# Attention in an adaptive-norm transformer block: the order of one unit's matmuls, written out in four blocks of two key tiles

## The chip, the core and the metric

The kernel runs on one core of one Trainium2 chip. The metric is the device time of one execution in microseconds (us). The kernel before takes 4075.78 us, the median of three runs (4074.69 to 4077.95).

## The reference

A transformer block (8 sequences of 1024 tokens, 512 features, 16 heads of 32) with modulated layer norms, and a modulated RMS norm behind it. Everything is float32. What the change touches is the softmax attention and its projection:

```python
h = layernorm(x, g1, be1) * (1.0 + scale_msa) + shift_msa
q, k, v = split_heads(h @ Wqkv + bqkv)                 # (8, 16, 1024, 32) each
attn = softmax(einsum('blhd,bmhd->bhlm', q, k) * 32 ** -0.5)
out = einsum('bhlm,bmhd->blhd', attn, v).reshape(8, 1024, 512)
x = x + gate_msa * (out @ Wproj + bproj)
h = layernorm(x, g2, be2) * (1.0 + scale_mlp) + shift_mlp
x = x + gate_mlp * (gelu(h @ W1 + b1) @ W2 + b2)
return rmsnorm(x) * (1.0 + scale) + shift              # scale, shift from a quantised projection
```

## The kernel before

Three stages follow each other: norm and QKV (to about 645 us), attention with its projection (to about 2560 us), MLP and the last norm. Each engine has one instruction stream, written out in the same nested loops, and semaphores tie the streams together. Only the attention stage and its seams are changed.

**A unit** of attention is four heads (128 features) of one sequence and one half of its queries (512 columns); there are `NU` = 64 units, `u` below. A unit has eight key tiles of 128 keys, `kt`. Its pieces, with the letter that the order strings use for them:

- `m`, a **maximum**: one 128x512 matmul of scores with the queries on the output's partitions (`pe_maximum`, L527) into one of **three** PSUM banks `SMAX`, and a VectorE reduction over it (`dve_maximum`, L817). 32 of them give the softmax shift of one later unit. A maximum may be written only when the reduction three places earlier in the ring has read its bank (`pe.wait_ge(dve_smax, at.turn - 2)`).
- `!`, the **send**: PE transposes the 16 maxima (L535, one turn of the same ring), VectorE negates them in two parts (L833, L836), and SyncE writes them as two more rows of the next unit's `q_stack`.
- `s`, a **score**: the same product with keys on the partitions and the shift in it (`pe_score`, L989) into one of three banks `ST`; ScalarE takes its exponential into `probs` (L1121). 32 per unit, four (one per head) for each key tile.
- **values** (`pe_values`, L1002): probabilities times V, four matmuls of 32 output rows each, one per head, that share the array in column tiles. As fp32 they run in two passes, so that the profile has 8 records for one key tile. **Denominators** (`pe_denominators`, L1018) are the same form against ones: number 0 and 1 for the last two key tiles, number 2 for `prob_sum`, the sum over the six others that GpSimd adds up (L1235, L1241; five additions of 128x2048 for a unit). "Column-tile products" below are both of these; a unit has eight values and three denominators.
- the **projection** of one token tile, 12 matmuls of 128x512 (L1029, L1031, L1033) into `DEN_BANK`, `PROJ_LAG` = 9 units late. ScalarE and GpSimd split its operand (`act_project` L1086, `pool_project` L1212), and VectorE gates its result (`dve_gate`, L1172).
- ScalarE empties the value bank (`act_weigh`, L1093); VectorE turns the denominators round, inverts, spreads and applies them (L1139, L1145, L1150, L1162).

**The order before** stands in a table for four steps of two key tiles, each in two halves:

```python
ORDER = (("mssm*mssm", "mssmm*mssmm"), ("mssm*mssm", "mssm*ssm"),
         ("mssm*ssm", "mssm*ssm"), ("mssm*!mssm", "mssmm*mssm"))
```

At a `*` PE does the step's other work (`pe_step_work`): two values; two denominators; one denominator and one value; one value three times; two values; and in the last half the whole projection. So the column-tile products of a unit stand in seven groups. `LEAD` = 9 maxima of a unit run ahead of its predecessor's send.

Of the kernel before, what the change touches and what calls it, by code (L numbers as in the profile page):

```python
# [7 lines left out]
def build_block(nc, t, out):  # L8
# [33 lines left out]
    STEPS = KT // 2  # L42
    LAST = STEPS - 1


    ORDER = (("mssm*mssm", "mssmm*mssmm"), ("mssm*mssm", "mssm*ssm"),
             ("mssm*ssm", "mssm*ssm"), ("mssm*!mssm", "mssmm*mssm"))
    LEAD = sum(x.count("m") for x in ORDER[-1])
# [11 lines left out]
    with whole:  # L60
# [104 lines left out]
        probs = [s2(f"probs{i}", [P, GH, 2, CH]) for i in range(3)]  # L165
# [104 lines left out]
        def slot(u, s):  # L270
            return (u * STEPS + s) % len(probs)

        def maxima_at(u, n):

            return u * N_MAX + n < NU * N_MAX

        def sums_done(u, s):
            return 5 * u + (1, 3, 5)[s]
# [135 lines left out]
        def ring_of_send(u):  # L414

            if u == 0:
                return N_MAX
            return min(N_MAX * (u + 1) + 2, N_MAX * NU) + u
# [510 lines left out]
        def sp_attention(sp):  # L929
# [7 lines left out]
            for u in range(NU):  # L937
# [16 lines left out]
                for s in range(STEPS):  # L954
                    for hs in range(2):
                        for what in ORDER[s][hs]:
                            if what == "!":
                                if u + 1 < NU:
                                    send_max(sp, u + 1)
                            elif what == "*" and (s, hs) == (0, 0):  # L960
                                if u and tile - 1 >= 0:
                                    store_gated(sp, tile - 1)
                                if half == 0 and G + 1 < NGRP:
                                    if u:
                                        sp.wait_ge(pe_pv, 8 * u)
                                    load_values(sp, G + 1)
# [13 lines left out]
        def pe_score(pe, u, s, h, j):  # L980
            G = u // NCH
            kt = 2 * s + j
            n = u * 32 + s * 8 + h * 2 + j
            if s == 0 and h == 0 and j == 0:
                pe.wait_ge(a_m[u % 3], 32 * (u // 3 + 1))
                pe.wait_ge(pool_ones, min(G, 1) + 1)
# [5 lines left out]
        def pe_values(pe, u, s, j):  # L992
            G = u // NCH
            kt = 2 * s + j
            if j == 0:
                pe.wait_ge(act_exp, u * 32 + s * 8 + 8)
# [4 lines left out]
            for h in range(GH):  # L1001
                i = pe.matmul(psum[h * HD:(h + 1) * HD, PV_BANK, :],  # L1002
                              v_group[G % 2][:, kt, h * HD:(h + 1) * HD],
                              probs[slot(u, s)][:, h, j, :], start=kt == 0, stop=kt == KT - 1)
            i.then_inc(pe_pv, 1)

        def pe_denominators(pe, u, n):
            term = prob_sum[u % 2] if n == 2 else probs[slot(u, LAST)][:, :, n, :]
            if n == 0:

                if u - PROJ_LAG >= 0 and u < NU:
# [3 lines left out]
            if n == 2:  # L1015
                pe.wait_ge(pool_sum, sums_done(u, 2))
# [4 lines left out]

        def pe_project(pe, n, bank):
            hi, lo = attn_hi[n % 2], attn_lo[n % 2]
            pe.wait_ge(act_ahi, n + 1)
            pe.wait_ge(pool_alo, n + 1)
            if n == 0:
                pe.wait_ge(dve_wprojlo, 1)
            for k in range(KD):
                pe.matmul(psum[:, bank, :], hi[:, k, :], wproj_hi[:, k, :], start=k == 0,  # L1029
                          stop=False)  # L1030
                pe.matmul(psum[:, bank, :], hi[:, k, :], wproj_lo[:, k, :], start=False,  # L1031
                          stop=False)
                i = pe.matmul(psum[:, bank, :], lo[:, k, :], wproj_hi[:, k, :], start=False,  # L1033
                              stop=k == KD - 1)
            i.then_inc(pe_proj2, 1)

        def pe_step_work(pe, u, s, hs):
            tile = u - PROJ_LAG
            if (s, hs) == (0, 0):
                if u:  # L1040
                    pe_values(pe, u - 1, LAST, 0)
                    pe_values(pe, u - 1, LAST, 1)
            elif (s, hs) == (0, 1):
                if u:
                    pe_denominators(pe, u - 1, 0)
                    pe_denominators(pe, u - 1, 1)
            elif s in (1, 2):
                if (s, hs) == (1, 0) and u:
                    pe_denominators(pe, u - 1, 2)
                pe_values(pe, u, s - 1, hs)  # L1050
            elif (s, hs) == (3, 0):
                pe_values(pe, u, 2, 0)
                pe_values(pe, u, 2, 1)
            elif tile >= 0:
                pe.wait_ge(dve_attn, u)
                pe_project(pe, tile, DEN_BANK)

        def pe_attention(pe, at):

            pe.wait_ge(dve_evict1, NC * 12)  # L1060
            for u in range(NU):
                for s in range(STEPS):
                    for hs in range(2):
                        n = 0
                        for what in ORDER[s][hs]:
                            if what == "s":
                                pe_score(pe, u, s, 2 * hs + n // 2, n % 2)
# [733 lines left out]
```

## Time and profile before

| | before |
|---|---|
| median of three runs | 4075.78 us |
| the profiled execution | 4073.34 us, span 4071.6 us |
| granted TensorE clock, mean | 0.993 |
| PE busy | 3995.4 us (98%) |
| VectorE, ScalarE, GpSimd busy | 2473.4, 1795.4, 1923.4 us |
| TENSOR_REDUCE of a maximum | 2048 times, 683 ns |
| exponential | 2048 times, 599 ns |
| GpSimd addition for `prob_sum` | 256 + 64 times, 4593 and 4589 ns |

PE means matmuls, PEld the loads of their stationary operands, which overlap them. Matmuls are pipelined: one of 128x512 is recorded with about 390 ns and the next starts about 230 ns after it, so that work on PE is counted from start to start. A matmul whose operand load came late is recorded with about 500 ns: it really starts about 0.11 us after its record does. An idle time of PEld with a releaser behind it is a wait of the load, and PE shows it only as such a longer record or a longer step to the next.

### The profile page before, as it was taken

The numbers are of one execution on the slowest core, as the hardware profiler recorded it, in microseconds if no ns is written. First come the engines' busy times: TensorE is split into PE (matmuls) and PEld (weight loads), VectorE is DVE, ScalarE is ACT, GpSimd is POOL, SyncE is SP. The second block draws the span as 40 slices with busy tenths as digits, with TensorE's granted clock in tenths as the row PEclk, the third lists the DMA queues.
The fourth block names the chain that finished last, engine by engine and source line by source line (L and its number), as shares of the span: only waits on it lengthen the run. The fifth ranks groups of instructions, "written<-read, shape, count | busy, mean of one in ns | idle before, by whom it ended". The sixth has DMA issues, their size and how long they took to land.

```text
span 4071.6 us, 51447 instructions
## 1 busy us (share of the span) xinstructions
PE 3995.4 (98%) x19723; PEld 2648.5 (65%) x19723; DVE 2473.4 (61%) x4020; ACT 1795.4 (44%) x3220; POOL 1923.4 (47%) x530
## 2 busy tenths in 40 slices
PE   8999999999999999999999999799999999999998
PEld 6778875445455455454455544588888888888886
DVE  3665557887777777777777775234445443344442
ACT  2222224665565555655555556333333333333332
POOL 1000005888788787887887878632211122231111
PEclk9999999999999999999999999999999999999999
DMA  5444463233323323323323330411110111201110
GB/s 199 175 173 176 183 210 102 53 73 76 75 64 82 78 53 84 76 55 84 74 65 74 74 78 26 142 55 42 34 42 34 42 39 50 62 34 42 34 42 21
DMA packets 184993, 323.70 MB, mean 80 GB/s; under 512 B 14452, under 2 KB 53428, under 8 KB 184748
## 3 DMA queue, kind: packets, MB, share of 16 engines
q1 hardware_dynamic: 184748, 320.41, 27.7%
q8 instruction: 156, 2.56, 0.3%
q14 instruction: 89, 0.73, 0.1%
HBM read 201.77 MB, written 117.54 MB: 78 GB/s over the span
## 4 chain that ended last, share of the span: by engine, by line
PE 94%; DVE 1%; DMA 1%; issue 1%; POOL 1%; ACT 1%; SPq 0%; POOLq 0%; ACTq 0%; DVEq 0%
PE psum L527 13%; PE psum L989 13%; PE psum L1002 12%; PE psum L428 10%; PE psum L430 9%; PE psum L429 9%; PE psum L1510 6%; PE psum L1514 6%; PE psum L1512 6%; PE psum L1018 4%; PE psum L1029 1%; PE psum L1031 1%; PE psum L1033 1%; PE psum L1472 1%; PE psum L463 1%
## 5 line engine op out<-in xcount | busy, mean ns | idle before, releaser
L817 DVE TENSOR_REDUCE max_part<-psum 128x1 f32<-128x512 f32 x2048 | 1298.6, 683 | 351.6 <-PE psum L527 340.8
L1121 ACT ACTIVATE probs<-psum 128x512 f32<-128x512 f32 x2048 | 1071.6, 599 | 686.1 <-PE psum L989 683.8
L1241 POOL TENSOR_TENSOR prob_sum<-prob_sum,probs 128x2048 f32<-128x2048 f32 x256 | 1175.8, 4593 | 111.7 <-ACT probs L1121 92.5
L1643 DVE TENSOR_TENSOR g_parts<-g_full,g_parts 128x512 fp32r<-128x512 f32 x256 | 311.7, 1217 | 776.0 <-ACT g_parts L1552 776.0
L527 PE MATMUL psum<-k_stack,q_stack 96*128 96x512 f32 x2048 | 758.2, 419 | 3.0 <-DVE max_part L817 1.3
L989 PE MATMUL psum<-q_stack,k_stack 98*128 98x512 f32 x2048 | 675.7, 411 | 4.9 <-DMA q_stack<-negmax_lo 2.5
L527 PEld LDWEIGHTS psum<-k_stack,q_stack 96*128 96x128 f32 x2048 | 387.5, 189 | 295.2 <-DVE max_part L817 235.9
L989 PEld LDWEIGHTS psum<-q_stack,k_stack 98*128 98x128 f32 x2048 | 372.1, 189 | 290.9 <-ACT probs L1121 250.2
L1548 ACT ACTIVATE g_full<-psum,cols 128x512 f32<-128x512 f32 x256 | 176.5, 690 | 823.4 <-PE psum L430 823.0
L1710 POOL TENSOR_TENSOR y_out<-y_out,rows 128x512 f32<-128x512 f32 x64 | 82.4, 1289 | 947.4 <-DVE y_out L1681 947.4
L1002 PE MATMUL psum<-probs,v_group 128*32 128x512 f32 x4096 | 517.4, 600 | 0.9 <-ACT probs L1121 0.9
L1235 POOL TENSOR_TENSOR prob_sum<-probs 128x2048 f32<-128x2048 f32 x64 | 293.7, 4589 | 254.6 <-ACT probs L1121 254.6
L1510 PE MATMUL psum<-w_hi,g_parts 128*128 128x512 f32 x1024 | 406.0, 396 | 0.0
L428 PE MATMUL psum<-h_hi,w_hi 128*128 128x512 f32 x1024 | 402.5, 393 | 1.7 <-ACT g_parts L1552 1.7
L1512 PE MATMUL psum<-w_lo,g_parts 128*128 128x512 f32 x1024 | 403.5, 394 | 0.0
L1514 PE MATMUL psum<-w_hi,g_parts 128*128 128x512 f32 x1024 | 403.4, 394 | 0.0
L430 PE MATMUL psum<-h_hi,w_lo 128*128 128x512 f32 x1024 | 401.4, 392 | 0.0
L429 PE MATMUL psum<-h_lo,w_hi 128*128 128x512 f32 x1024 | 401.1, 392 | 0.0
L1002 PEld LDWEIGHTS psum<-probs,v_group 128*32 128x32 f32 x4096 | 100.2, 108 | 231.7 <-issue 145.6
L428 PEld LDWEIGHTS psum<-h_hi,w_hi 128*128 128x128 f32 x1024 | 192.3, 188 | 48.5 <-issue 3.8
L1514 PEld LDWEIGHTS psum<-w_hi,g_parts 128*128 128x128 f32 x1024 | 192.3, 188 | 45.2
L1512 PEld LDWEIGHTS psum<-w_lo,g_parts 128*128 128x128 f32 x1024 | 192.4, 188 | 43.8
(152 smaller groups left out, 4731.7 us busy)
## 6 DMA issues: line engine op xcount, KB each, us to landing
qk_parts<-qk_out SPq DMA_DIRECT2D x128, 512.0 KB, 2.8
k_stack<-qk_parts SPq DMA_DIRECT2D x96, 512.0 KB, 7.0
q_stack<-qk_parts SPq DMA_DIRECT2D x192, 256.0 KB, 9.4
x_in<-in_x SPq DMA_DIRECT2D x16, 1024.0 KB, 5.4
v_rows<-v_out SPq DMA_DIRECT2D x64, 256.0 KB, 2.0
v_group<-v_rows SPq DMA_DIRECT2D x32, 512.0 KB, 12.1
gated_attention<-gated SPq DMA_DIRECT2D x64, 256.0 KB, 4.6
x<-in_x SPq DMA_DIRECT2D x16, 1024.0 KB, 7.9
```

The lines of the kernel that those rows point to most:

```text
L428: pe.matmul(dst, lh, rh, start=n == 0, stop=False)
L429: pe.matmul(dst, lh, rl, start=False, stop=False)
L430: last = pe.matmul(dst, ll, rh, start=False, stop=n == len(terms) - 1)
L527: pe.matmul(psum[:, SMAX[at.turn % 3], :], q_stack[u % 3][0:PARTS, h, i * P:(i + 1) * P], k_stack[G % 2][0:PARTS, h, kh * CH:(kh + 1) * CH ...
L817: dve.reduce_max(max_part[:, n:n + 1], psum[:, SMAX[at.turn % 3], :], AX.X).then_inc(dve_smax, 1)
L989: pe.matmul(psum[:, ST[n % 3], :], k_stack[G % 2][0:ROWS, h, kt * P:(kt + 1) * P], q_stack[u % 3][0:ROWS, h, :], start=True, stop=True).th ...
L1002: i = pe.matmul(psum[h * HD:(h + 1) * HD, PV_BANK, :], v_group[G % 2][:, kt, h * HD:(h + 1) * HD], probs[slot(u, s)][:, h, j, :], start=kt ...
L1121: act.activation(probs[slot(u, s)][:, h, j, :], psum[:, ST[k % 3], :], ACT.Exp, scale=SCALE).then_inc(act_exp, 1)
L1241: pool.tensor_tensor(prob_sum[u % 2][:, :, :], prob_sum[u % 2][:, :, :], probs[slot(u, s)][:, :, j, :], ALU.add).then_inc(pool_sum, 1)
L1510: pe.matmul(psum[:, ACC[m], :], gp[:, 0, cut], w2_hi[piece][:, at, :], start=i == 0, stop=False)
L1512: pe.matmul(psum[:, ACC[m], :], gp[:, 0, cut], w2_lo[piece][:, at, :], start=False, stop=False)
L1514: pe.matmul(psum[:, ACC[m], :], gp[:, 1, cut], w2_hi[piece][:, at, :], start=False, stop=i == KM - 1).then_inc(pe_down, 1)
```

## The change

The unit's order becomes one string of four blocks. Each block scores two key tiles and ends in all its column-tile products (`V` values, `D` denominators); the projection's products, `j`, stand one by one in the last block. The other letters place work of the other engines: `g` gate, `w` weigh, `a` `act_project`, `t r p n` turn, reciprocal, spread, normalise.

The send stands at the middle of the unit, so `LEAD` becomes 16. The probabilities have a ring of six single key tiles in place of three pairs, and values run two key tiles behind the scores (`PV_LAG`). The sums wait and run per key tile, and `pool_project` stands behind the second addition. In the seam to the MLP the first projection of the tail moves ahead of the denominators, and the second ahead of denominator 2.

```diff
-    ORDER = (("mssm*mssm", "mssmm*mssmm"), ("mssm*mssm", "mssm*ssm"),
-             ("mssm*ssm", "mssm*ssm"), ("mssm*!mssm", "mssmm*mssm"))
-    LEAD = sum(x.count("m") for x in ORDER[-1])
+    ORDER = ("msgmsmsmsamsmsmsmsVVDD", "mswmsmsmsmsmsmsmsVVD!", "msmstsmsrmspsmsmsVV",
+             "nmsmsmsmjsjmjsjmjsjmjsjmjsjmjmjVV")
+    LAST = KT - 1
+    SUMMED = KT - 2
+    AHEAD = 0
+    LEAD = N_MAX + AHEAD - "".join(ORDER).split("!")[0].count("m")
+    PV_LAG = 2
+    RING = 6
...
-        probs = [s2(f"probs{i}", [P, GH, 2, CH]) for i in range(3)]
+        probs = [s2(f"probs{i}", [P, GH, CH]) for i in range(RING)]
...
+                for what in "".join(ORDER):
...
+                    elif what == "V":
+                        if values >= PV_LAG:
+                            pe_values(pe, u, values - PV_LAG)
+                        elif u:
+                            pe_values(pe, u - 1, values - PV_LAG + KT)
+                        values += 1
+                    elif what == "D" and u:
+                        pe_denominators(pe, u - 1, dens)
+                        dens += 1
+                    elif what == "j" and u - PROJ_LAG >= 0:
+                        if products == 0:
+                            pe.wait_ge(dve_attn, u)
+                        pe_project_product(pe, u - PROJ_LAG, DEN_BANK, products)
+                        products += 1
...
+                        if h == 0 and k >= RING:
+                            pu, pk = divmod(k - RING, KT)
+                            act.wait_ge(pe_pv, k - RING + 1)
+                            if pk >= SUMMED:
+                                act.wait_ge(pe_den, 3 * pu + pk - SUMMED + 1)
+                            else:
+                                act.wait_ge(pool_sum, sums_done(pu, pk))
...
         def pe_tail(pe):
             at = TAIL[0]
-            pe_values(pe, NU - 1, LAST, 0)
-            pe_values(pe, NU - 1, LAST, 1)
-            pe.wait_ge(dve_gated, at)
+            for kt in range(KT - PV_LAG, KT):
+                pe_values(pe, NU - 1, kt)
+            pe.wait_ge(dve_smax, FIRST_TAIL)
+            pe_project(pe, at, tail_bank(at))
             pe_denominators(pe, NU - 1, 0)
             pe_denominators(pe, NU - 1, 1)
-            pe.wait_ge(dve_smax, FIRST_TAIL)
-            pe_project(pe, at, tail_bank(at))
+            pe_project(pe, at + 1, tail_bank(at + 1))
             pe_denominators(pe, NU - 1, 2)
```

On PE, a unit's start before (L527 maxima, L989 scores, L1002 values, L1018 denominators; a row's x8 counts matmuls in the program):

```order
L1002 MATMUL psum<-probs_116,v_group_103 32x512 x8
L527 MATMUL psum<-k_stack_111,q_stack_101 128x512
L989 MATMUL psum<-q_stack_112,k_stack_111 128x512 x2
L527 MATMUL psum<-k_stack_111,q_stack_101 128x512 x2
L989 MATMUL psum<-q_stack_112,k_stack_111 128x512 x2
L527 MATMUL psum<-k_stack_111,q_stack_101 128x512 x2
L1018 MATMUL psum<-probs_116,ones 32x512 x8
```

The same place on PE after the change, the end of the first block (L532 maxima, L992 scores, L1003 values, L1019 denominators):

```order
L532 MATMUL psum<-k_stack_100,q_stack_112 128x512
L992 MATMUL psum<-q_stack_102,k_stack_111 128x512
L532 MATMUL psum<-k_stack_100,q_stack_112 128x512
L992 MATMUL psum<-q_stack_102,k_stack_111 128x512
L1003 MATMUL psum<-probs_115,v_group_113 32x512 x4
L1003 MATMUL psum<-probs_116,v_group_113 32x512 x4
L1019 MATMUL psum<-probs_115,ones 32x512 x4
L1019 MATMUL psum<-probs_116,ones 32x512 x4
```

Before, products stood behind every four to six maxima and scores; now 16 of these run in strict alternation, and two values and two denominators follow together.

VectorE before, from the gate (L1172) to the send (L833, L836) and on to the next gate, with the runs of reductions (L817) between its other work:

```order
L817 TENSOR_REDUCE max_part<-psum 128x1 x9
L1172 TENSOR_TENSOR gated_125<-psum,gates_other 128x512
L817 TENSOR_REDUCE max_part<-psum 128x1 x10
L1139 STREAM_TRANSPOSE den_turned<-psum 128x512
L817 TENSOR_REDUCE max_part<-psum 128x1 x4
L1145 RECIPROCAL den_inv<-den_turned 128x16
L817 TENSOR_REDUCE max_part<-psum 128x1 x3
L1150 STREAM_TRANSPOSE psum<-den_inv 128x512
L817 TENSOR_REDUCE max_part<-psum 128x1 x3
L1162 TENSOR_TENSOR attn_last<-weighted_130,psum 128x512
```

VectorE after the change (L822 is the reduction, L1162 the gate, L838 and L841 the send, L1129, L1135, L1140 and L1152 turn, reciprocal, spread and normalise):

```order
L1162 TENSOR_TENSOR gated_128<-psum,gates_last 128x512
L822 TENSOR_REDUCE max_part<-psum 128x1 x15
L829 TENSOR_REDUCE max_q<-max_part 128x16
L838 TENSOR_SCALAR negmax_hi<-psum 16x128
L841 SCALAR_TENSOR_TENSOR negmax_lo<-psum,negmax_hi 16x128
L822 TENSOR_REDUCE max_part<-psum 128x1 x2
L1129 STREAM_TRANSPOSE den_turned<-psum 128x512
L822 TENSOR_REDUCE max_part<-psum 128x1
L1135 RECIPROCAL den_inv<-den_turned 128x16
L822 TENSOR_REDUCE max_part<-psum 128x1
L1140 STREAM_TRANSPOSE psum<-den_inv 128x512
```

The gate has moved behind the first maximum of the first block, and send, turn, reciprocal and spread have moved together into the third block, among six maxima.

## Rows read from the trace of the kernel before

**Rows 1.** The page: the chain that ended last, by engine.
```profile
PE 94%; DVE 1%; DMA 1%; issue 1%; POOL 1%; ACT 1%; SPq 0%; POOLq 0%; ACTq 0%; DVEq 0%
```
**Rows 2.** Timeline of PE: start us, us, engine line op, tiles, count.
```profile
2011.58 1.92 PE L1002 MATMUL psum<-probs,v_group 128*32 128x512 f32 x16
2013.44 0.50 PE L527 MATMUL psum<-k_stack,q_stack 96*128 96x512 f32 x1
2013.78 0.63 PE L989 MATMUL psum<-q_stack,k_stack 98*128 98x512 f32 x2
...
2022.32 0.63 PE L989 MATMUL psum<-q_stack,k_stack 98*128 98x512 f32 x2
...
2023.25 0.65 PE L989 MATMUL psum<-q_stack,k_stack 98*128 98x512 f32 x2
2023.74 0.39 PE L527 MATMUL psum<-k_stack,q_stack 96*128 96x512 f32 x1
2024.06 1.06 PE L1002 MATMUL psum<-probs,v_group 128*32 128x512 f32 x8
2025.06 0.74 PE L989 MATMUL psum<-q_stack,k_stack 98*128 98x512 f32 x2
...
2036.96 0.39 PE L1029 MATMUL psum<-wproj_hi,attn_hi 128*128 128x512 f32 x1
...
2039.45 0.39 PE L1033 MATMUL psum<-wproj_hi,attn_lo 128*128 128x512 f32 x1
```
**Rows 3.** Timeline of PE: a send in units 0, 1, 10 and 61.
```profile
669.65 0.28 PE L535 MATMUL psum<-ident,max_q 128*16 128x128 f32 x1
697.58 0.28 PE L535 MATMUL psum<-ident,max_q 128*16 128x128 f32 x1
951.32 0.28 PE L535 MATMUL psum<-ident,max_q 128*16 128x128 f32 x1
2485.75 0.28 PE L535 MATMUL psum<-ident,max_q 128*16 128x128 f32 x1
```
**Rows 4.** Timeline of VectorE, around one gate and one idle start.
```profile
2012.54 0.68 DVE L1172 TENSOR_TENSOR gated<-psum,gates_other 128x512 f32<-128x512 f32 x1
2013.97 3.19 DVE L817 TENSOR_REDUCE max_part<-psum 128x1 f32<-128x512 f32 x5 [0.75 <-PE psum L527]
...
2021.35 0.71 DVE L1139 STREAM_TRANSPOSE den_turned<-psum 128x512 f32<-128x512 f32 x1
```
**Rows 5.** Timeline of PE in unit 0: three maxima behind a full ring.
```profile
671.42 1.49 PE L527 MATMUL psum<-k_stack,q_stack 96*128 96x512 f32 x3
672.74 0.63 PE L989 MATMUL psum<-q_stack,k_stack 98*128 98x512 f32 x2
```
**Rows 6.** Timeline of VectorE at the same place, behind the send.
```profile
670.48 3.66 DVE L817 TENSOR_REDUCE max_part<-psum 128x1 f32<-128x512 f32 x6
```
**Rows 7.** Timeline of ScalarE: the weigh and four exponentials.
```profile
2013.57 0.60 ACT L1093 ACTIVATE weighted<-psum 128x512 f32<-128x512 f32 x1 [1.21 <-PE psum L1002]
2014.21 2.06 ACT L1121 ACTIVATE probs<-psum 128x512 f32<-128x512 f32 x4
```
**Rows 8.** Timeline of GpSimd over one unit.
```profile
2019.64 4.59 POOL L1235 TENSOR_TENSOR prob_sum<-probs 128x2048 f32<-128x2048 f32 x1 [4.30 <-ACT probs L1121]
2024.20 1.27 POOL L1212 TENSOR_TENSOR attn_lo<-attn_other,attn_hi 128x512 fp32r<-128x512 f32 x1
2026.76 18.66 POOL L1241 TENSOR_TENSOR prob_sum<-prob_sum,probs 128x2048 f32<-128x2048 f32 x4 [1.29 <-ACT probs L1121]
```
**Rows 9.** The waits, 1000 to 2400 us: who for whom, us, times, longest.
```profile
PEld psum L527 <- DVE max_part L817: 168.0, 323, 0.8
```
**Rows 10.** Timeline of PE, unit 63 and the seam behind it.
```profile
2520.00 0.86 PE L989 MATMUL psum<-q_stack,k_stack 98*128 98x512 f32 x3
...
2528.17 0.50 PE L989 MATMUL psum<-q_stack,k_stack 98*128 98x512 f32 x1 [0.22 <-ACT probs L1121]
...
2557.63 1.06 PE L1018 MATMUL psum<-prob_sum,ones 128*32 128x512 f32 x8
```

More of the change, by code:

```diff
@@ L953, in sp_attention @@
                     load_gates(sp, b)
[L954 to L966, printed above, removed]
+                values = 0
+                for what in "".join(ORDER):
+                    if what == "!" and u + 1 < NU:
+                        send_max(sp, u + 1)
+                    elif what == "V":
+                        values += 1
+                        if values == PV_LAG and half == 0 and G + 1 < NGRP:
+                            if u:
+                                sp.wait_ge(pe_pv, KT * u)
+                            load_values(sp, G + 1)
+                    elif what == "g" and tile >= 1:
+                        store_gated(sp, tile - 1)
         def load_gates(sp, b):
@@ L1020, in pe_denominators, with pe_project_product @@
             i.then_inc(pe_den, 1)
-        def pe_project(pe, n, bank):
[L1023 to L1056, printed above, removed]
+        def pe_project_product(pe, n, bank, m):
+            hi, lo = attn_hi[n % 2], attn_lo[n % 2]
+            if m == 0:
+                pe.wait_ge(act_ahi, n + 1)
+                pe.wait_ge(pool_alo, n + 1)
+                if n == 0:
+                    pe.wait_ge(dve_wprojlo, 1)
+            k, kind = divmod(m, 3)
+            left, right = ((hi, wproj_hi), (hi, wproj_lo), (lo, wproj_hi))[kind]
+            i = pe.matmul(psum[:, bank, :], left[:, k, :], right[:, k, :], start=m == 0,
+                          stop=m == 3 * KD - 1)
+            if m == 3 * KD - 1:
+                i.then_inc(pe_proj2, 1)
+        def pe_project(pe, n, bank):
+            for m in range(3 * KD):
+                pe_project_product(pe, n, bank, m)
         def pe_attention(pe, at):
@@ new lines, in act_attention @@
+                scores = 0
+                for what in "".join(ORDER):
+                    if what == "s":
+                        kt, h = divmod(scores, GH)
+                        k = u * KT + kt
+                        if h == 0 and k >= RING:
[5 more added lines that the diff above has]
+                                act.wait_ge(pool_sum, sums_done(pu, pk))
+                        n = k * GH + h
+                        act.wait_ge(pe_st, n + 1)
+                        act.activation(probs[slot(u, kt)][:, h, :], psum[:, ST[n % 3], :],
+                                       ACT.Exp, scale=SCALE).then_inc(act_exp, 1)
+                        scores += 1
+                    elif what == "w" and u:
+                        act_weigh(act, u - 1)
+                    elif what == "a" and tile >= 0:
+                        act_project(act, tile)
@@ L1380, in dve_tail @@
             dve.wait_ge(pe_den, 3 * NU)
[L1381 to L1382 removed]
+            dve.wait_ge(pool_sum, sums_done(NU - 1, SUMMED - 1))
+            for n, tile in enumerate(TAIL[2:], 2):
                 dve_gate(dve, tile, tail_bank(tile))
```

157 lines of the change are left out of this document (57 added, 100 removed).

## The prediction

> **What bounds the kernel now.** I read the page first: PE is busy for 98% of the span (the table above) and makes 94% of the chain that ended last [rows 1]. So only time on PE counts, and time of another engine only where it holds PE up. Next the sends, one per unit, as a clock: 951.32 to 2485.75 us is 51 units with a projection, 30.09 us each; 697.58 to 951.32 is eight without one and one with, so (253.74 - 30.09) / 8 = 27.96 for those [rows 3]. What fills a unit comes from the timeline of PE, start to start [rows 2].
>
> - Four maxima and scores from 2022.32 to 2023.25: 0.233 each. Projection: 11 steps from 2036.96 to 2039.45, 0.226 each.
> - A group of two column-tile products lasts 1.86 until the next matmul (2011.58 to 2013.44), a group of one 1.00 (2024.06 to 2025.06): 0.86 for one, and 0.14 once per group. The step into a group is 0.32 (2023.74 to 2024.06) and the first step behind one 0.34 (2013.44 to 2013.78, whose first record is 0.50 long, an operand load that could not run ahead), in place of 0.233. A group thus costs 0.09 + 0.14 + 0.105 = 0.33 beyond its products.
>
> The unit before: 64 x 0.233 + 12 x 0.226 + 11 x 0.86 + 7 x 0.33 = 14.9 + 2.7 + 9.45 + 2.3 = 29.4. The other 0.65 are waits that show only as long records and steps: the loads of maxima wait for a reduction 323 times and 168 us in 1400 us [rows 9], most of it ahead of time and so free.
>
> The Trainium skill (TensorEngine Tiling (Array Packing), Key Properties) says that changing the tiling mode drains the engine; by that rule alone fewer groups are a pure gain, and the sum would be rival A below. The same page (PSUM Bottleneck) warns that tiling speeds up TensorE and not the emptying of PSUM; the terms below, from rows, go that way.
>
> **The rule of the ring.** Three banks stand between PE and VectorE. Count a maximum from its effective start E (record plus 0.105 where it follows a group). Its reduction starts at E + 0.43: 2013.44 + 0.105 to 2013.97 [rows 2, 4]. One lasts 0.69 after an idle start, 0.67 to 0.68 in a queue; six take 3.66, so the step is (3.66 - 0.67) / 5 = 0.60 [rows 6]. The gate takes 0.68 [rows 4], in a queue one more step of 0.60. What does PE see when it waits? In unit 0 the third reduction ends at 670.48 + 1.20 + 0.67 = 672.35, and the matmul behind the third waiting maximum starts at 672.74 [rows 5, 6], so that the maximum's own E was 672.51: E of a maximum is at least F + 0.16, F the end of the reduction three turns earlier. Scores obey the same rule with ScalarE: step (2.06 - 0.60) / 3 = 0.49 [rows 7], and in unit 63 the fourth score of a run starts 1.19 after the first [rows 10], which is 0.43 + 0.60 + 0.16.
>
> A pair of maximum and score costs PE 0.47 and VectorE 0.60. A run of strict pairs therefore uses up three banks of slack and then goes at VectorE's pace. Before, a group stood behind every two or three maxima and gave VectorE its time back; now eight maxima run before one.
>
> **The change, block by block** (t from the block's first record, F and E as above; all other steps at 0.233).
>
> - Removed: three groups, 3 x 0.33 = -1.00 per unit, and the old waits, -0.65.
> - Block 1, eight pairs and the gate behind the first maximum. E1 = 0.105, reduction 0.54 to 1.23, gate from 1.14, second reduction 1.74 to 2.42, then F3, F4, F5 = 3.02, 3.62, 4.22. E5 = 2.58 instead of 1.97, E8 = F5 + 0.16 = 4.38 instead of 3.37. Wait: +1.0. The block is 4.38 + 0.23 + 0.32 + four products (1.86 + 2 x 0.86 = 3.57) = 8.5; VectorE is done at 6.0, so that each long group does empty its queue, but with nothing left to gain from it.
> - Block 2, eight pairs without the gate: F5 = 3.62, E8 = 3.78, +0.4. ScalarE's weigh stands behind the first exponential and pushes the second to 1.76 to 2.36; score 5 then waits for 2.52 instead of 2.22, score 7 for 3.50, and the block's last score is at 4.0 to 4.13 [rows 7]. That is +0.45 in all; length 7.1 with three products.
> - Block 3: the send takes the ring's first turn. Its first reduction starts 0.83 behind the transpose (669.65 to 670.48) [rows 3, 6], F1 = 1.50, F2 = 2.10, then the turn (0.71, rows 4) to 2.74 and F3 = 3.33. E6 must wait for it: 3.49 instead of 2.92. +0.57. The exponentials add nothing beyond it (score 6 at 2.52, inside the same wait). Length 5.9.
> - Block 4: normalise is done at 0.6, behind the third block's last reduction; the fourth maximum may start at 1.43 and would at 1.50; from there on a projection product stands between two pieces, 0.69 or more per maximum but for the last. No wait. 0.105 + 18 x 0.233 + 12 x 0.226 + 0.09 + 1.86 = 9.0.
>
> Sum 8.5 + 7.1 + 5.9 + 9.0 = 30.5, against 30.09: as a difference -1.00 - 0.65 + 1.0 + 0.45 + 0.57 = +0.37 to +0.40. Bounds: if the gate hid wholly (it would have to wait for nothing and cost no step) block 1 falls to 0.4, and the unit to -0.2; if the weigh and the turn each cost a full step more, it is +0.6. I take +0.38, since every term uses a duration that the rows show in the same engine state.
>
> In units 1 to 8 nothing is gated or projected: block 1 waits 0.4, block 4 has ten maxima in pairs (E10 = F7 + 0.16 = 4.97, wait +1.0, length 7.15), sum 28.06 against 27.96: +0.1 each.
>
> GpSimd: five additions and the split are 4.59 + 1.27 + 18.66 = 24.5 of a unit [rows 8]. From the unit's start: sum 1 from 5.7 to 10.3 (key tile 1's last exponential), sum 2 from 11.3, the split until 17.2, the rest until 31. The tile that needs the sum 5 buffer is scored at 30.5 + 10, the earliest other one (key tile 6 over tile 0) at 22 over 10.3. Slack of 9 or more; no wait. The split is done 4 ahead of the first `j` at 23. Keys and queries for the maxima two units on are now wanted at 15.6 instead of about 23 into a unit, but their loads leave SyncE some 3 us before its start, with the last score; the page has 7.0 and 9.4 us to landing. Free.
>
> **The seams.** LEAD moves seven maxima into the end of the QKV stage, where PE is the bound: 7 x 0.233 = +1.6. They come out of unit 62, whose last two blocks then run at ScalarE's pace (eight scores in a run: 3.27 + 0.32 instead of 3.92 with maxima), as all of unit 63. There GpSimd sets the end: its sums finish some 30.3 into unit 63, the split 1.3 later, then projection, two denominators, projection, denominator 2: done at about 40.6, against 38.7 from the same unit's first scores at 2520.0 to 2558.7, the last record's end [rows 10]. Everything behind hangs on that last one: +2.
>
> **Total.** 52 units x 0.38 = +19.8; unit 9 (no gate yet) -0.2; units 0 to 8 about +1.1; QKV end +1.6; seam +2. +24.3 on the profiled execution's 4073.34 (its span 4071.6 and 1.7 around it) is 4097.6. The median of the runs lies 2.4 above that execution, so I forecast **4100 us**, +0.6%; its own range is 4090 to 4112.
>
> **Rivals.**
>
> - A, faster: the saved groups count whole and the waits stay at 0.65. Mechanism: the load of the waiting maximum is taken while scores run, so that the ring's delay is absorbed; point of decision: it needs four banks' worth of slack, or reductions at 0.47 like the pair. For it: the old loads wait 168 us and PE shows almost nothing of it [rows 9]. Against: there a group follows within three maxima, and rows 5 show the wait in full when none does. Price -1.00 x 62 + 3.6 for the seams: 4017.
> - B, no change: a wait costs only until the release, with the load hidden (0.11 less). That takes 0.11 from three blocks, +0.05 per unit, with the seams +6 to +8: 4083. For it: several waits in a row could overlap; against: rows 5 and 10.
> - C, slower still: the third block's VectorE backlog reaches the fourth, and the projection waits for the normalise (needed by 1.7, done by 0.6 by my sum). If reciprocal and spread each wait 0.5 for the step before, block 3 waits 0.6 more: 4135. The rows of before have no such chain without maxima between.
>
> That the change does not do what it says is excluded: the program's order has the four groups and the single `j`.
>
> **Chances.** Forecast 0.68, A 0.12, B 0.12, C 0.08. A difference of 0.2% (8 us) is about what a measurement of this kernel can tell from none. Faster 0.14 (A, and some of B), same 0.12, slower 0.74. The range leaves out most of A and part of C: 4068 to 4120.
>
> **What would show it.** In the changed profile the sends of units 10 to 61 stand 30.4 to 30.5 apart; the eighth maximum of block 1 starts 4.3 to 4.4 behind the first, in records of about 0.5; block 2 about 7.1 long, block 3 5.9, block 4 9.0; reductions in block 1 in one queue with the gate, without idle time; loads of maxima that wait for reductions well over 168 us in 1400. If the sends stand 29.1 apart, the ring's rule fails and A is right. If the unit is right and the total is not, the seams are.

## The result, and the profile after

The changed kernel takes 4105.71 us (median of 4 runs, 4105.40 to 4106.81) against 4075.79 for the one before (4 runs): a ratio of 1.0073, with a 95% interval of 1.0056 to 1.0091. It is slower by 30 us, where 24 were forecast. The profiled execution took 4106.81 us with a span of 4105.0; its mean granted clock was 0.992.

The page: the span, the busy line, and the chain that ended last. PE is busy for the same 97 to 98% as before, but its share of the chain has gone from 94% [rows 1] to 87%, and VectorE's from 1% to 4%.

```profile
span 4105.0 us, 51828 instructions
PE 4001.0 (97%) x19723; PEld 2688.5 (65%) x19723; DVE 2439.9 (59%) x4020; ACT 1791.7 (44%) x3220; POOL 1920.1 (47%) x530
PE 87%; DVE 4%; issue 3%; ACT 2%; DMA 2%; POOL 1%; SPq 0%; ACTq 0%; POOLq 0%; DVEq 0%
```

The unit's pace, from the timeline of PE: the sends of units 10 and 61, and one in between from which the rows below go on. 2505.22 - 947.87 is 51 units of 30.54; before it was 30.09 [rows 3].

```profile
947.87 0.28 PE L540 MATMUL psum<-ident,max_q 128*16 128x128 f32 x1
...
1986.14 0.28 PE L540 MATMUL psum<-ident,max_q 128*16 128x128 f32 x1
...
2505.22 0.28 PE L540 MATMUL psum<-ident,max_q 128*16 128x128 f32 x1
```

One unit's blocks, from the timeline of PE (L532 maxima, L992 scores, L1003 values, L1019 denominators, L1033 projection). Block 3 runs from the send at 1986.14 to 1992.01, block 4 to 2001.06, block 1 of the next unit to 2009.58.

```profile
1992.01 0.50 PE L532 MATMUL psum<-k_stack,q_stack 96*128 96x512 f32 x1
...
1999.21 1.92 PE L1003 MATMUL psum<-probs,v_group 128*32 128x512 f32 x16
2001.06 0.50 PE L532 MATMUL psum<-k_stack,q_stack 96*128 96x512 f32 x1
2001.40 0.40 PE L992 MATMUL psum<-q_stack,k_stack 98*128 98x512 f32 x1
...
2003.54 0.50 PE L532 MATMUL psum<-k_stack,q_stack 96*128 96x512 f32 x1 [0.35 <-DVE max_part L822]
...
2005.33 0.50 PE L532 MATMUL psum<-k_stack,q_stack 96*128 96x512 f32 x1
2005.68 0.40 PE L992 MATMUL psum<-q_stack,k_stack 98*128 98x512 f32 x1
2006.01 1.92 PE L1003 MATMUL psum<-probs,v_group 128*32 128x512 f32 x16
2007.75 1.90 PE L1019 MATMUL psum<-probs,ones 128*32 128x512 f32 x16
2009.58 0.50 PE L532 MATMUL psum<-k_stack,q_stack 96*128 96x512 f32 x1
```

The fifth maximum starts 2.48 behind the first, the eighth 4.27, each in a record of 0.50. VectorE in the same block, from its timeline: one reduction, the gate, seven reductions, with no idle time between them.

```profile
2001.60 0.69 DVE L822 TENSOR_REDUCE max_part<-psum 128x1 f32<-128x512 f32 x1 [1.69 <-PE psum L532]
2002.21 0.68 DVE L1162 TENSOR_TENSOR gated<-psum,gates_other 128x512 f32<-128x512 f32 x1
2002.81 4.27 DVE L822 TENSOR_REDUCE max_part<-psum 128x1 f32<-128x512 f32 x7
```

Averaged over 46 units the blocks last 8.51, 7.10, 5.88 and 9.05. The waits from 1000 to 2400 us (who for whom, us in total, times, longest), which answer to [rows 9]:

```profile
PEld psum L532 <- DVE max_part L822: 130.0, 315, 0.8
...
PEld psum L992 <- ACT probs L1113: 82.6, 327, 0.7
```

Where the 33.4 us between the two spans lie, from the same landmarks of both timelines: first score +3.9 (646.63 to 650.54; 2.0 of it lies ahead of the first early maximum, where the programs do the same), unit 0 +0.6, units 1 to 8 +0.6, units 10 to 61 +23.4, unit 62 -0.5, unit 63 and the seam up to the last denominators +5.9 (38.23 to 44.16), all behind them -0.35.

### The profile page after: what moved, and what is told of

The parts are those of the page before. It is cut to its first block, busy times and chain, and to the rows that moved or that the text cites. A ratio compares the mean times of both kernels' runs of the same rounds, so it can differ in the third digit from the quotient of the medians.

```text
span 4105.0 us, 51828 instructions
## 1 busy us (share of the span) xinstructions
PE 4001.0 (97%) x19723; PEld 2688.5 (65%) x19723; DVE 2439.9 (59%) x4020; ACT 1791.7 (44%) x3220; POOL 1920.1 (47%) x530
## 3 DMA queue, kind: packets, MB, share of 16 engines
q1 hardware_dynamic: 184748, 320.41, 27.2%
## 4 chain that ended last, share of the span: by engine, by line
PE 87%; DVE 4%; issue 3%; ACT 2%; DMA 2%; POOL 1%; SPq 0%; ACTq 0%; POOLq 0%; DVEq 0%
PE psum L1003 11%; PE psum L532 11%; PE psum L992 10%; PE psum L433 9%; PE psum L435 9%; PE psum L434 9%; PE psum L1493 6%; PE psum L1497 6%; PE psum L1495 6%; PE psum L1033 4%; PE psum L1019 4%; DVE max_part L822 2%; ACT probs L1113 1%; ACT weighted L1087 1%; DVE gated L1162 1%
## 5 line engine op out<-in xcount | busy, mean ns | idle before, releaser
L822 DVE TENSOR_REDUCE max_part<-psum 128x1 f32<-128x512 f32 x2048 | 1279.0, 677 | 347.6 <-PE psum L532 343.7
L1113 ACT ACTIVATE probs<-psum 128x512 f32<-128x512 f32 x2048 | 1087.1, 615 | 789.4 <-PE psum L992 786.6
L532 PE MATMUL psum<-k_stack,q_stack 96*128 96x512 f32 x2048 | 874.4, 427 | 22.4 <-DVE max_part L822 19.2
L992 PE MATMUL psum<-q_stack,k_stack 98*128 98x512 f32 x2048 | 828.5, 411 | 11.5 <-DMA q_stack<-negmax_lo 2.5
L532 PEld LDWEIGHTS psum<-k_stack,q_stack 96*128 96x128 f32 x2048 | 387.3, 189 | 346.3 <-DVE max_part L822 196.4
L992 PEld LDWEIGHTS psum<-q_stack,k_stack 98*128 98x128 f32 x2048 | 387.8, 190 | 174.6 <-ACT probs L1113 123.9
L1003 PE MATMUL psum<-probs,v_group 128*32 128x512 f32 x4096 | 493.9, 600 | 0.0
L1216 POOL TENSOR_TENSOR prob_sum<-probs,probs 128x2048 f32<-128x2048 f32 x64 | 292.5, 4571 | 265.0 <-ACT probs L1113 265.0
L1003 PEld LDWEIGHTS psum<-probs,v_group 128*32 128x32 f32 x4096 | 107.1, 109 | 237.6 <-issue 166.1
```

Of the source, the lines that this page charges most:

```text
L532: pe.matmul(psum[:, SMAX[at.turn % 3], :], q_stack[u % 3][0:PARTS, h, i * P:(i + 1) * P], k_stack[G % 2][0:PARTS, h, kh * CH:(kh + 1) * CH ...
L822: dve.reduce_max(max_part[:, n:n + 1], psum[:, SMAX[at.turn % 3], :], AX.X).then_inc(dve_smax, 1)
L992: pe.matmul(psum[:, ST[n % 3], :], k_stack[G % 2][0:ROWS, h, kt * P:(kt + 1) * P], q_stack[u % 3][0:ROWS, h, :], start=True, stop=True).th ...
L1003: i = pe.matmul(psum[h * HD:(h + 1) * HD, PV_BANK, :], v_group[G % 2][:, kt, h * HD:(h + 1) * HD], probs[slot(u, kt)][:, h, :], start=kt = ...
L1113: act.activation(probs[slot(u, kt)][:, h, :], psum[:, ST[n % 3], :], ACT.Exp, scale=SCALE).then_inc(act_exp, 1)
```

## The experiments

Ten kernels ran, each an edit of the changed one. The runs of before beside them gave 4076.4, 4075.8 and 4074.3. "Unit" is the spacing of the sends of units 10 to 61. "Own work" is the sum of the prediction with the projection's step as measured here when it is interleaved, 0.234: 64 x 0.233 + 12 x 0.234 + 11 x 0.86 = 27.2, and 0.33 for each group. What a unit takes beyond that is waits. For before, with its step of 0.226, they come to 0.7 (the prediction, 0.65).

The theory at the start was the prediction's: reductions hold the ring of three banks, so that the unit is set by VectorE's turns alone. Its rivals: ScalarE's exponentials hold PE as much, so that relieving VectorE gives little; and the groups saved are worth less than 0.33.

| kernel | us | ratio to before (95%) | unit | own work | waits |
|---|---|---|---|---|---|
| before | 4075.8 | 1 | 30.09 | 29.4 | 0.7 |
| changed | 4105.7 | 1.0073 (1.0056 to 1.0091) | 30.54 | 28.5 | 2.0 |
| gate_late | 4078.2 | 1.0004 (0.9995 to 1.0014) | 30.02 | 28.5 | 1.5 |
| turn_early | 4099.5 | 1.0057 (1.0040 to 1.0073) | 30.43 | 28.5 | 1.9 |
| half_reduce | 4058.1 | 0.9956 (0.9941 to 0.9971) | 29.90 | 28.5 | 1.4 |
| half_exp | 4101.1 | 1.0064 (1.0041 to 1.0087) | 30.50 | 28.5 | 2.0 |
| both_half | 3982.4 | 0.9776 (0.9734 to 0.9818) | 28.64 | 28.5 | 0.1 |
| seven_groups | 4063.1 | 0.9971 (0.9960 to 0.9982) | 29.79 | 29.5 | 0.3 |
| block_projection | 4148.9 | 1.0181 (1.0164 to 1.0198) | 31.38 | 28.4 | 3.0 |
| tail_before | 4103.7 | 1.0068 (1.0047 to 1.0088) | 30.54 | 28.5 | 2.0 |
| spread_j_only | 4050.9 | 0.9938 (0.9923 to 0.9953) | 29.56 | 28.5 | 1.1 |
| spread | 4013.1 | 0.9845 (0.9830 to 0.9859) | 29.08 | 28.5 | 0.6 |

**gate_late.** The gate goes behind block 1's eight reductions.

```diff
-    ORDER = ("msgmsmsmsamsmsmsmsVVDD",
+    ORDER = ("msmsmsmsamsmsmsmsgVVDD",
```

> The gate stands behind block 1's eighth maximum instead of behind the first; nothing else moves. Ring theory (PE waits for VectorE's pace through three banks): block 1's wait falls from 1.0 to 0.4, with at most 0.1 back at the denominators, which now wait for a later gate. Units 30.0 to 30.1 us apart instead of 30.54, the kernel 4074 to 4082 us. Rival (strict alternation of maxima and scores itself costs PE, whatever VectorE does): no change, 4106.

The unit is 0.52 shorter. The timeline of PE shows block 1's first and eighth maximum 3.68 us apart instead of 4.27, and the block 7.97 long:

```profile
1980.99 0.50 PE L532 MATMUL psum<-k_stack,q_stack 96*128 96x512 f32 x1
...
1984.67 0.50 PE L532 MATMUL psum<-k_stack,q_stack 96*128 96x512 f32 x1
...
1988.96 0.50 PE L532 MATMUL psum<-k_stack,q_stack 96*128 96x512 f32 x1
```

VectorE's rows of that block: the gate's 0.68 now lie beside the products.

```profile
1981.53 4.88 DVE L822 TENSOR_REDUCE max_part<-psum 128x1 f32<-128x512 f32 x8 [1.69 <-PE psum L532]
1986.33 0.68 DVE L1162 TENSOR_TENSOR gated<-psum,gates_other 128x512 f32<-128x512 f32 x1
```

So one VectorE instruction's place decides 27 us: nearly the whole loss of the change.

**turn_early.** All three denominators stand in block 1, so that turn and reciprocal can go from block 3 to the end of block 2; only the spread is left among block 3's maxima.

```diff
-    ORDER = ("msgmsmsmsamsmsmsmsVVDD", "mswmsmsmsmsmsmsmsVVD!", "msmstsmsrmspsmsmsVV",
+    ORDER = ("msgmsmsmsamsmsmsmsVVDDD", "mswmsmsmsmsmsmsmstrVV!", "msmssmsmspsmsmsVV",
```

> Denominator 2 joins block 1's group, turn and reciprocal move behind block 2's last maximum, and only the spread stays in block 3. Ring theory: block 3's wait for the reduction behind the turn goes (0.57), of which exponentials keep 0.1 to 0.3; block 1 grows and block 2 shrinks by one product, 0.86. Units 30.1 to 30.25 apart, the kernel 4081 to 4092. Rival (alternation): no change.

The miss: the unit fell by 0.11 and block 3 only from 5.88 to 5.77. With the reductions out of the way, its scores wait for the exponentials instead. The fourth score (the first row, from the timeline of PE in block 3) has the record of a load that waited; beside it ScalarE, by its own timeline, has the eight exponentials of the block in one queue (the row holds the last seven of them).

```profile
1982.65 0.50 PE L992 MATMUL psum<-q_stack,k_stack 98*128 98x512 f32 x1
```

```profile
1982.49 3.54 ACT L1113 ACTIVATE probs<-psum 128x512 f32<-128x512 f32 x7
```

**half_reduce, half_exp, both_half.** Half of the load is taken from one engine or from both. The reduction reads 256 of each maximum's 512 columns, or the exponential works on 256 of 512, or both. In the two kernels with half exponentials ScalarE also fills the other half of the probabilities once, with 12 copies ahead of unit 0; the unit's pace is taken behind them.

```diff
-            dve.reduce_max(max_part[:, n:n + 1], psum[:, SMAX[at.turn % 3], :],
+            dve.reduce_max(max_part[:, n:n + 1], psum[:, SMAX[at.turn % 3], 0:CH // 2],
```

```diff
-                        act.activation(probs[slot(u, kt)][:, h, :], psum[:, ST[n % 3], :],
+                        act.activation(probs[slot(u, kt)][:, h, 0:CH // 2],
+                                       psum[:, ST[n % 3], 0:CH // 2],
```

> Leaves out half of each maximum: the reduction reads 256 of its 512 columns, all matmuls stay. A reduction's step should be about 0.35 to 0.4 instead of 0.60, below the 0.47 of a pair. Ring theory: all waits for VectorE go, the ones for exponentials stay (0.3 to 0.6 a unit): units 28.7 to 29.1 apart, the kernel 4005 to 4030. Rival (alternation): units stay at 30.5 and the kernel at 4106. If groups are worth less than 0.33 each, the unit stays above 29.1.

The unit kept 1.4 of its 2.0 us of waits: 28.7 to 29.1 was expected and 29.90 came; for the kernel, 4005 to 4030 and 4058.1. The grouped lines from 1000 to 2400 us have the reduction at 416 ns (677 in the changed kernel), and VectorE idle for 534.5 us ahead of it, so it isn't VectorE that holds PE:

```profile
L822 DVE TENSOR_REDUCE max_part<-psum 128x1 f32<-128x256 f32 x1498 | 606.3, 416 | 534.5 <-PE psum L532 506.6
```

ScalarE's timeline in block 1 shows what does: its queue has no gap, and `act_project` takes a place in it between two runs of exponentials.

```profile
1997.17 2.06 ACT L1113 ACTIVATE probs<-psum 128x512 f32<-128x512 f32 x4 [3.16 <-PE psum L992]
1999.09 0.65 ACT L1080 ACTIVATE attn_hi<-attn_other 128x512 fp32r<-128x512 f32 x1
1999.62 2.09 ACT L1113 ACTIVATE probs<-psum 128x512 f32<-128x512 f32 x4
```

PE's timeline in that block: the eighth maximum starts nearly unhindered (3.45 behind the first, 3.37 without any wait), and the eighth score is the one with the record of 0.50, at 3.97.

```profile
1996.32 0.50 PE L532 MATMUL psum<-k_stack,q_stack 96*128 96x512 f32 x1
...
1999.77 0.39 PE L532 MATMUL psum<-k_stack,q_stack 96*128 96x512 f32 x1
2000.29 0.50 PE L992 MATMUL psum<-q_stack,k_stack 98*128 98x512 f32 x1
```

That led to the theory of two rings, each of which alone nearly holds the unit, and to the next two.

> The exponentials take 256 of their 512 columns (the other half of the probabilities keeps what 12 copies put there at the start of attention, some 8 us of ScalarE, so half of the output is not attention's); reductions and all matmuls as in the changed kernel. Theory after the first runs (VectorE and ScalarE each hold the blocks by themselves, so that taking away one leaves most of the wait): VectorE's waits stay, units 30.3 to 30.5 apart. Rival (ScalarE is the engine that counts, VectorE only rides along): 29.0 or less.

> Both at once: reductions and exponentials over half the columns, same 12 copies. Both theories' waits go: the unit should come down to PE's own work, 64 x 0.2335 + 12 x 0.234 + 22 x 0.43 + 4 x 0.334 = 28.5, with at most 0.2 left: units 28.4 to 28.7 apart. Rival (the order costs PE something that no other engine's pace explains, such as alternating operands): above 29.3.

Both came as expected: halving the exponentials alone gives 0.04, halving the reductions alone 0.64, both together 1.90, which is all but 0.14 of the waits. The gains do not add: 1.2 of the 1.9 is to be had only when both engines are relieved.

By block, averaged over 50 units from the timelines of PE (us):

| kernel | block 1 | block 2 | block 3 | block 4 |
|---|---|---|---|---|
| changed | 8.51 | 7.10 | 5.88 | 9.05 |
| half_exp | 8.51 | 7.05 | 5.87 | 9.06 |
| half_reduce | 7.98 | 7.10 | 5.77 | 9.06 |
| both_half | 7.59 | 6.66 | 5.34 | 9.06 |
| seven_groups (below) | 7.85 | 7.01 | 5.88 | 9.06 |

So what the two engines hold is 0.92, 0.44, 0.54 and nothing, block by block. Of block 1's 0.92 the reductions alone give 0.53; of blocks 2 and 3 neither engine alone gives more than 0.11.

In the waits from 1000 to 2400 us one engine's row grows when the other is relieved. Half_exp, whose reductions held loads for 130.0 us in the changed kernel:

```profile
PEld psum L532 <- DVE max_part L822: 192.2, 452, 0.8
```

and half_reduce, whose exponentials held them for 82.6 us:

```profile
PEld psum L992 <- ACT probs L1113: 133.4, 469, 0.7
```

**seven_groups.** The seven groups come back. Single `j` and late turn stay; the gate stands one maximum later than in the changed kernel.

```diff
-    ORDER = ("msgmsmsmsamsmsmsmsVVDD", "mswmsmsmsmsmsmsmsVVD!", "msmstsmsrmspsmsmsVV",
+    ORDER = ("msmsgmsmsVamsmsmsmsVDD", "mswmsmsmsVmsmsmsmsVD!", "msmstsmsVrmspsmsmsV",
```

> The changed kernel with its column-tile products spread again: one value behind every eight pieces, and the groups of two denominators and of one value and denominator as before, so seven groups; the projection stays one by one in block 4. Ring theory: 3 x 0.33 = +1.0 for the groups, the waits of 2.0 fall to about 0.1 to 0.3: units 29.5 to 29.8 apart, the kernel 4050 to 4068, below the one before. Rival (groups are what counts, waits don't follow them): units 31.5, the kernel about 4160.

Three more groups cost PE 1.0 and save 1.7 of waits: 0.75 less per unit than the changed kernel. But the run doesn't show that the grouping is what loses. By the table above 0.66 of the 0.75 lie in block 1, where the gate has moved too, and gate_late's 0.53 in that block needed no regrouping. In blocks 2 and 3 only the grouping differs: block 2 is 0.09 shorter and block 3 the same, so that a group's price and the wait that it saves nearly cancel. What the grouping of block 1 costs with the gate where it was, no run shows; with four groups and the gate late (gate_late) the unit is 30.02, 0.23 above seven_groups.

**block_projection.** The fourth block as the others: all pieces, then the twelve projection products in a row.

```diff
-             "nmsmsmsmjsjmjsjmjsjmjsjmjsjmjmjVV")
+             "nmsmsmsmsmsmsmsmsmmjjjjjjjjjjjjVV")
```

> The projection's twelve products stand in one block behind block 4's maxima and scores again, the four groups stay. Ring theory: ten maxima in pairs wait by VectorE's pace, E10 = 4.97 instead of 4.07, +0.9, and the products alone take 0.226 instead of 0.234 (-0.1): block 4 about 9.9, units 31.3 apart, the kernel 4140 to 4155. Rival (one-by-one placing is worth nothing): units 30.4 to 30.5.

The unit is 0.85 longer, all of it in block 4 (9.90 instead of 9.05). Within the changed order the single `j` is the part that gains: as the only one of the four blocks the fourth has no wait, because a product stands where VectorE needs its time.

**tail_before.** The seam to the MLP in the order of before: denominators 0 and 1, projection, denominator 2, and only then the next projection.

```diff
-            pe.wait_ge(dve_smax, FIRST_TAIL)
-            pe_project(pe, at, tail_bank(at))
             pe_denominators(pe, NU - 1, 0)
             pe_denominators(pe, NU - 1, 1)
-            pe_project(pe, at + 1, tail_bank(at + 1))
+            pe.wait_ge(dve_smax, FIRST_TAIL)
+            pe_project(pe, at, tail_bank(at))
             pe_denominators(pe, NU - 1, 2)
```

> Only the seam's order of before is restored: the last unit's denominators 0 and 1 ahead of the first tail projection. They then run while PE waits for the split, and the clock may stay up: the last denominator ends 2 to 4 us earlier counted from unit 63's first score (44.2 in the changed kernel, 38.2 before). The rest of the loss there is unit 63 itself. Kernel 4102 to 4104. Rival (the seam's loss is all in unit 63's blocks): no change in the stretch behind the last score.

From unit 63's first score to the last denominators' end it is 37.86 instead of 44.16: 6.3 less, where 2 to 4 were expected. In the total that cannot be told: 4103.7 against 4105.7, intervals that overlap, and this kernel's profiled execution reached its first score 3.8 later, at 654.34, with the granted clock at 0.50 from 603.9 to 610.7. The timeline of PE shows the seam of the changed kernel:

```profile
2575.31 3.64 PE L1003 MATMUL psum<-probs,v_group 128*32 128x512 f32 x32
2582.14 0.47 PE L1033 MATMUL psum<-wproj_hi,attn_hi 128*128 128x512 f32 x1 [3.19 <-POOL attn_lo L1196]
...
2583.59 0.63 PE L1033 MATMUL psum<-wproj_hi,attn_lo 128*128 128x512 f32 x1
2584.02 0.63 PE L1033 MATMUL psum<-wproj_hi,attn_hi 128*128 128x512 f32 x1
...
2586.65 1.92 PE L1019 MATMUL psum<-probs,ones 128*32 128x512 f32 x16
2588.51 0.50 PE L1033 MATMUL psum<-wproj_hi,attn_hi 128*128 128x512 f32 x1
...
2591.45 1.06 PE L1019 MATMUL psum<-prob_sum,ones 128*32 128x512 f32 x8
```

and that of tail_before:

```profile
2579.15 3.64 PE L1003 MATMUL psum<-probs,v_group 128*32 128x512 f32 x32
2582.61 1.90 PE L1019 MATMUL psum<-probs,ones 128*32 128x512 f32 x16
2586.03 0.47 PE L1033 MATMUL psum<-wproj_hi,attn_hi 128*128 128x512 f32 x1 [1.51 <-POOL attn_lo L1196]
...
2588.96 1.06 PE L1019 MATMUL psum<-prob_sum,ones 128*32 128x512 f32 x8
```

In both the first projection starts 33.8 behind the unit's first score, when GpSimd's split is done. In the changed order the two denominators that could have filled the wait (1.86) and a second projection (2.94) then stand ahead of the last denominators, and the first projection takes 4.51 instead of 2.93, at the lower clock. 1.86 + 2.94 + 1.58 = 6.4.

**spread_j_only and spread.** If each place where VectorE lags wants a product, the projection should lie in two blocks. `J` stands for the last four products of the tile that the unit before has begun. The first kernel does that alone, the second also regroups: three denominators in block 1 with `a`, `w` and `g` behind its values, none in block 2, turn and reciprocal ahead of block 3, and the seam of before.

```diff
# spread_j_only
+    ORDER = ("msmsmsJmsamsJmsJmsJmsgVVDD", "mswmsmsmsmsmsmsmsVVD!", "msmstsmsrmspsmsmsVV",
+             "nmsmsmsmsjmsjmjsjmjsjmsjmmjVV")
# spread
+    ORDER = ("msmsJmsmsJmsmJsmsJmsmVVawgDDD", "msmssmsmsmsmsmstrVV!", "msmssmsmsmspmsmsVV",
+             "nmsmsmsmjsmjjsmjsmjjsmjsmjVV")
...
+                    elif what == "J" and u - 1 - PROJ_LAG >= 0:
+                        pe_project_product(pe, u - 1 - PROJ_LAG, DEN_BANK, 3 * KD - LATE + late)
+                        late += 1
```

> Only four of the twelve projection products move from block 4 into the next unit's first block, the gate behind the last of them. Ring theory: they fit into block 1's wait of 1.0, so that block 1 stays at 8.5 and block 4 loses 4 x 0.234: units 29.5 to 29.7 apart, the kernel 4055 to 4066. Rival (the waits follow from the group's length, not from the run ahead of it): units stay at 30.5.

> The version that the runs point to: four projection products move into the next unit's first block (the gate behind them), act_project, weigh and all three denominators into block 1's group, turn and reciprocal behind block 2's last maximum, maxima 9, 7, 7 and 9 per block, and the seam's order of before. Ring theory with both engines: VectorE has no run of more than it can take, and ScalarE's eight exponentials hold blocks 2 and 3 to about 3.95 before their groups. Blocks about 9.5, 5.8, 5.8 and 7.9, units 29.0 apart (28.8 to 29.3), the kernel 4012 to 4035. Rival (one of the two engines' waits cannot be moved off PE, only shifted): units stay above 29.7, no faster than before.

The units came as expected, 29.56 and 29.08; the first kernel's total was 4 us below its range, 3.2 of them in the seam (40.94 instead of 44.16), where the first projection ran at the full clock. Spread is the fastest kernel that does the whole work: 0.9845 of before (0.9830 to 0.9859) and 92.6 us below the changed one. Of the changed kernel's unit 0.97 goes with the four products and the gate (0.52 by gate_late, which leaves some 0.45 for the products) and 0.49 with the regrouping and the other moved letters together; the seam gives 8.2 (35.95 instead of 44.16). Its loads wait for reductions and exponentials, from 1000 to 2400 us:

```profile
PEld psum L993 <- ACT probs L1117: 74.3, 347, 0.6
...
PEld psum L533 <- DVE max_part L823: 49.6, 95, 0.8
```

## Why the prediction was right, point by point

- **The ring's rule held.** The blocks were forecast at 8.5, 7.1, 5.9 and 9.0 and last 8.51, 7.10, 5.88 and 9.05. Block 1's eighth maximum was to start effectively at 4.38; its record starts at 4.27, and 0.105 of the load makes 4.38. The unit is 0.45 over before, where I had taken 0.38: the projection's step, which I had at 0.226, is 0.234 where the products stand singly, and 12 x 0.008 = 0.1 covers what is missing. Over 52 units that makes 23.4 instead of 19.8. The waits themselves were forecast at 1.0, 0.45, 0.57 and none, and both_half puts them at 0.92, 0.44, 0.54 and none.
- **The gate** was 0.6 of block 1's term (4.38 against 3.78 without it). Gate_late measures 0.52.
- **The groups' 0.33** was right within what can be seen: with it both_half's unit leaves 0.14 unexplained, and seven_groups, with three groups more, 0.30. In neither is the price measured apart from the waits.
- **Block 3's term was right and its reason only half.** The prediction said that the exponentials add nothing beyond the reductions. They add little, but they stand right behind: turn_early took the turn out of the way and got 0.11 of the 0.57. The same holds for blocks 1 and 2 (half_reduce). Where two waits end close together, the sum over the later one is a good forecast of the time and a bad forecast of what an edit would give.
- **Units 0 to 8** were to give +1.1 and gave 1.1, but not as worked out. Half of it is unit 0, one of whose maxima waits for queries: "free" was wrong there. What that wait adds to the unit isn't measured by itself, since the granted clock is at half in both kernels there, but not for the same stretch (645.3 to 655.5 before, 651.2 to 658.0 now). From the timeline of PE:

```profile
665.26 0.50 PE L532 MATMUL psum<-k_stack,q_stack 96*128 96x512 f32 x1 [1.51 <-DMA q_stack<-qk_parts]
```

- **The seam** was mis-sized: +5.9 measured, +2 forecast. The prediction has 38.7 for before, counted from 2520.0; but the row there [rows 10] starts with scores of unit 62, and unit 63's first is at 2520.47, which makes it 38.2. For the changed kernel it has 40.6, and 44.16 came: GpSimd's last addition ended at 32.4, not 30.3, and the first projection ran at the lower clock, 1.6 more. The late addition is mostly the clock as well. In block_projection, whose unit 63 starts with the same matmuls in the same steps, the first group of values takes 1.92 and not 3.50; GpSimd's second addition starts 11.0 behind the unit's first score instead of 12.6, and the last one ends at 30.75. Half_reduce and spread_j_only, without a fall in that group, have 30.8 and 30.7; gate_late and tail_before, with it, 32.4 and 32.5. So two falls of the clock make up 3.2 of the 4 us that the forecast lacked. The order of events was as foretold.
- **The QKV end** was to cost +1.6. The first score comes 3.9 later, of which 2.0 precede any edit. From the first early maximum to the first score there are 49 maxima instead of 42, and the stretch takes 51.4 us instead of 49.5. In nine of the other kernels, whose QKV stage has the same matmuls, it takes 50.8 to 52.7, and in tail_before 55.4, with the fall of the clock told above. So the term is borne out at about 1.9, against one trace of before; and a few us of any total here are that stage's scatter.
- **The total** came nearer than its terms. The sum was +24.3 on the profiled executions, whose spans differ by 33.4: 4 are missing in the seam, 3.6 in the units, and 2.0 lie ahead of any edit. The medians differ by 30 only because before's profiled execution lay 2.4 below its median and the changed one's 1.1 above. That part is luck.
- **The waits of loads** were to be well over 168 us; they are 130.0. With those for exponentials, before 179.4 and now 82.6, the view has gone down by 135 us while a unit's waits on PE went up from 0.7 to 2.0. Before, the load waited ahead of time behind other matmuls; now the matmul waits with it (so I read the rows; no run isolates it). This view doesn't measure what PE loses. The spacing of the sends does.
- **Rival A** named what spread came near to: its unit of 29.1 is the 29.1 that A gave, by another way. The ring's delay isn't absorbed by scores; it has to be given products. **Rival B**, a wait without the load's 0.11, would have the waiting maximum in a record as long as the ones that don't wait, 0.39 or 0.40; it is 0.50, and the blocks' lengths hold the 0.11. **Rival C** fell: block 4 shows no wait for the normalise, and lasts 9.05.

The Trainium skill (TensorEngine Tiling (Array Packing), Key Properties) says that changing the tiling mode drains TensorE. The rows agree with it as far as they go: a group costs 0.33 beyond its products, 0.105 of which is the load behind it. No run shows the drain by itself. That fewer groups are a pure gain once nothing waits fits both_half, 28.64 with four groups, but no kernel with seven groups and no waits stands beside it. The Trainium skill's section PSUM Bottleneck, on the same page, advises to empty PSUM with ScalarE and VectorE both. This kernel does; the runs add that the two then need relief together (0.64 and 0.04 alone, 1.90 together).

## What to carry to other kernels

Where PE is busy for 98% of the time, count what each engine that empties its banks needs per piece (here 0.60 on VectorE and 0.49 on ScalarE against 0.47 of PE for the pair), and place the work that needs no emptying (values, denominators, projection) where their queues have filled. What needs no change of tiling mode, as the projection, goes in singly rather than at a block's end. A group in another tiling mode costs 0.33 here, a full ring 0.44 to 0.92 in a block, and in blocks 2 and 3 one more group saved hardly more than it cost. A long instruction of the emptying engine, such as the gate, is better ahead of a group of products than in a run of strict pairs: here 0.52 of a unit. When a stretch is held by two engines, halve both once before taking either's share for what it would give.

## What the runs showed of the hardware that was not expected

In unit 63 and the seam the granted clock fell behind short idle times of PE. The table by stretch of the changed kernel (start and end, length; busy time of PE, PEld, DVE, ACT, POOL with counts; granted clock, DMA share, GB/s):

```profile
2525.00:2548.30 23.30, 22.83 (x134) 10.29 (x133) 9.80 (x19) 13.74 (x27) 20.39 (x6) 1.00 0.01 4
2548.30:2552.50 4.20, 3.39 (x12) 1.42 (x8) 0.00 (x0) 3.52 (x8) 3.70 (x1) 0.99 0.13 52
2552.50:2557.70 5.20, 5.20 (x33) 1.16 (x32) 0.00 (x0) 1.02 (x3) 4.11 (x1) 0.68 0.00 0
...
2582.00:2592.50 10.50, 10.36 (x48) 5.92 (x48) 1.38 (x2) 0.00 (x0) 1.24 (x1) 0.84 0.06 25
```

At 2552.59 a group of 16 values takes 3.50 instead of 1.92, at the lower level (1.2 GHz), behind a stretch in which PE was idle for 0.8 of 4.2 us. The projection behind the idle 3.19 us starts in steps of 0.23 and goes over to steps of 0.43 about 1.0 us in, for some 3.5 us. The group of 16 alone cost 1.6. In before the clock was 1.00 over the same unit, from 2520.0 to 2558.7, with an idle time of 3.3 us ahead of its first projection.

The idle times do not decide it by themselves. Turn_early's unit 63 starts with the same matmuls and the same 3.39 us of work in 4.20, and its clock stays up:

```profile
2541.35:2545.55 4.20, 3.39 (x12) 1.42 (x8) 0.00 (x0) 3.51 (x8) 4.20 (x1) 1.00 0.13 52
```

```profile
2545.59 1.92 PE L1003 MATMUL psum<-probs,v_group 128*32 128x512 f32 x16
```

Block_projection and half_reduce have no fall there either; gate_late and tail_before do. The second fall is in gate_late too and not in tail_before, whose idle time ahead of the projection is 1.51 instead of 3.19. Why the clock falls in one kernel and not in another stays open.
